# Matmuls that nobody reads, put between the products of TensorE in a token, attention and expert kernel

## What is computed

```python
h = leaky_relu(batchnorm(conv2d(x, stem_w, stem_b, 4)))          # 96 channels, 24x24
offset = conv2d(h, off_w, off_b, 4)                              # 16 taps x (y, x) for each of 6x6 tokens
h = deform_conv(h, offset, dcn_w, dcn_b)                         # 4 bilinear corners per tap, then a product
h = leaky_relu(batchnorm(h))                                     # 36 tokens x 192
h = h + attention(layernorm(h))                                  # 12 heads, 64 random features exp(proj - |t|^2/2)
h = h + experts(layernorm(h))                                    # 1 of 3 experts per image, 192 -> 768 -> 192, gelu
```

## Time and profile before

| | us |
|---|---|
| runs of the kernel | 508.93, 511.91, 514.75 (median 511.91) |
| profiled execution, span | 511.0 |
| TensorE busy | 424.5 (83%) |
| TensorE weight loads | 298.8 (58%) |
| VectorE busy | 307.6 (60%) |
| ScalarE busy | 227.5 (45%) |
| GpSimd busy | 159.0 (31%) |
| chain that ended last | TensorE 64%, VectorE 12%, ScalarE 8%, issue 6% |

### The profile page before, as it was taken

How to read it: one execution, slowest core, us unless ns; L and a number is a source line. 1 busy time by engine, 2 the same in 40 slices (tenths; PEclk the granted TensorE clock), 3 DMA queues, 4 the chain that set the end, 5 groups by cost and what they waited for, 6 DMA issues and landing times.

```text
span 511.0 us, 7813 instructions
## 1 busy us (share of the span) xinstructions
PE 424.5 (83%) x2630; PEld 298.8 (58%) x2630; DVE 307.6 (60%) x1180; ACT 227.5 (45%) x548; POOL 159.0 (31%) x168
## 2 busy tenths in 40 slices
PE   4992546599778989998798899799779888988997
PEld 2571333466474558665765685466647675666576
DVE  4561538453345778955369885844569895458222
ACT  2373335433435675344333753626245652652520
POOL 3106757201436552006265440005365410000000
PEclk9996669559985589999889999699799999999999
DMA  5559844659725332077234430086244310000000
GB/s 137 138 144 269 207 133 120 186 181 228 210 62 142 94 90 81 1 186 217 64 108 114 140 98 2 1 210 192 69 133 107 98 47 1 0 1 2 17 1 17
DMA packets 60022, 54.27 MB, mean 106 GB/s; under 512 B 44242, under 2 KB 52335, under 8 KB 59983
## 3 DMA queue, kind: packets, MB, share of 16 engines
q0 software_dynamic: 9216, 28.32, 19.6%
q1 hardware_dynamic: 50336, 25.42, 19.4%
q10 hardware_dynamic: 431, 0.03, 0.1%
HBM read 38.70 MB, written 15.06 MB: 105 GB/s over the span
## 4 chain that ended last, share of the span: by engine, by line
PE 64%; DVE 12%; ACT 8%; issue 6%; another core or an unknown queue 3%; POOL 3%; DMA 2%; ACTq 1%; DVEq 0%; POOLq 0%
PE bank L899 7%; PE bank L871 6%; PE bank L668 6%; PE bank L593 4%; PE bank L574 4%; PE bank L878 4%; PE bank L809 3%; PE bank L790 3%; PE bank L604 3%; POOL ring L519 3%; PE bank L794 2%; PE bank L825 2%; PE bank L750 2%; PE bank L552 2%
## 5 line engine op out<-in xcount | busy, mean ns | idle before, releaser
L519 POOL DMA_INDIRECT ring<-cells,cell x144 | 146.5, 1018 | 221.6 <-DVE cell L1334 100.0
L1356 DVE SCALAR_TENSOR_TENSOR bank<-ring,corner,bank 128x96 f32<-128x96 f32 x224 | 52.9, 312 | 26.1 <-ACT bank L1074 22.9
L668 PE MATMUL bank<-w_dcn,shared 128*128 128x192 f32 x192 | 44.8, 376 | 21.4 <-ACT shared L1083 13.2
L1198 ACT ACTIVATE hid<-bank,b_up 128x288 f32<-128x288 f32 x72 | 32.1, 497 | 63.6 <-PE bank L878 55.8
L871 PE MATMUL bank<-xfT,w_up 128*128 128x288 f32 x144 | 47.9, 458 | 5.8 <-ACT hid L1198 3.5
L668 PEld LDWEIGHTS bank<-w_dcn,shared 128*128 128x128 f32 x192 | 34.9, 212 | 30.3 <-ACT shared L1083 18.0
L899 PE MATMUL bank<-w_down,hid 128*128 128x192 f32 x288 | 52.1, 332 | 0.0
L899 PEld LDWEIGHTS bank<-w_down,hid 128*128 128x128 f32 x288 | 46.2, 190 | 4.6 <-issue 4.4
L871 PEld LDWEIGHTS bank<-xfT,w_up 128*128 128x128 f32 x144 | 27.0, 208 | 15.4 <-ACT hid L1198 5.7
L1074 ACT ACTIVATE bank<-ring,corner 128x96 f32<-128x96 f32 x112 | 31.4, 336 | 6.7 <-DMA ring<-cells,cell 5.5
L574 PE MATMUL bank<-xt,w_stem 48*96 48x384 f32 x96 | 32.6, 774 | 1.2 <-DVE h L1373 1.2
(11 more groups left out here) (182 smaller groups left out, 699.0 us busy)
## 6 DMA issues: line engine op xcount, KB each, us to landing
cells<-ring SPq DMA_DIRECT2D x16, 864.0 KB, 8.1
xs<-in_x_dram SPq DMA_DIRECT2D x28, 108.0 KB
ring<-cells,cell POOLq DMA_INDIRECT x144
w_down<-in_L_ffn_W_dram SPq DMA_DIRECT2D x3, 576.0 KB, 7.1
hid<-in_L_tok_dcn_w_dram SPq DMA_DIRECT2D x1, 1152.0 KB, 7.6
w_up<-in_L_ffn_W_dram SPq DMA_DIRECT2D x3, 384.0 KB, 3.8
out_dram<-y SPq DMA_DIRECT2D x8, 96.0 KB, 2.2
w_up_rest<-in_L_ffn_W_dram SPq DMA_DIRECT2D x6, 96.0 KB, 4.2
```

Of the source, the lines that this page charges most:

```text
L519: pool.indirect_dma_start(ring[:, ring_slot(k), j, :], None, table[0:HALF_CELLS, :] if k < EARLY else table, bass.IndirectOffsetOnAxis(ap= ...
L668: mm = pe.matmul(tokens_out(t), samp[:, n % 2, i, :], w_dcn[:, CHUNKS * (k % QUADS) + i, :], start=(k % QUADS == 0 and i == 0), stop=(k % ...
L1198: act.activation(hid[:, e % 2, f, :], up_bank(g, n)[:, 0:TOK], ACT.Gelu, bias=b_up[:, n:n + 1]).then_inc(gelu_done, 1)
L1356: ins = dve.scalar_tensor_tensor(acc[:, k % 3, :, j, :] if c == 3 else part_sum, ring[:, ring_slot(k), j, C1 * c:C1 * (c + 1)].rearrange(" ...
```

## The change

A function `keep_warm(bank, count)` is new. It issues `count` matmuls with `ident` as the stationary operand and 384 columns of `w_dcn` as the moving one, into a PSUM bank. They wait for nothing, raise no semaphore, and what they write is never read.

```diff
+            def keep_warm(bank, count):
+                for _ in range(count):
+                    pe.matmul(ps[bank][:, 0:2 * C2], ident[:, :], w_dcn[:, 0:2, :].rearrange("p n c -> p (n c)"),
+                              start=True, stop=True)
...
             def dcn(g, has_last, has_next):
                 for k in range(BATCHES):
+                    if g == 0 and k >= 6:
+                        keep_warm(5, 1)
                     dcn_turn(g, k)
...
+                    if g == 0 and k == 5:
+                        keep_warm(5, 4)
                     dcn_products(g, k)
...
+                if g == 0:
+                    keep_warm(5, 1)
                 fold_tokens(g)
...
                     pe.wait_ge(kv_hi, 6 * g + (u + 1))
+                    if u == 2:
+                        keep_warm(7, 3)
                     if u >= 2:
                         pe.wait_ge(o_evac, 6 * g + (u - 1))
...
                 attend(g)
                 if has_last:
                     up_wide(g - 1, 2, 0)
+                else:
+                    keep_warm(7, 2)
                 channels(g, xa, xa_ready, t3_mm, TILES)
...
                     for s in range(2):
                         stem_x(2, s)
-                        stem_products(2, s)
+                        for j in range(3):
+                            stem_products(2, s, 2 * j, 2 * j + 2)
+                            keep_warm(0, 1)
```

## The result

On the chip of the first pair the changed kernel takes 532.3 us (median of 4; 529.0 to 536.6) and the kernel before 512.9 (median of 4). The ratio is 1.040, 95% interval 1.034 to 1.046: slower by 4%, where faster by 2% was forecast. Ratios here compare runs of the same state, so they can differ by some tenths of a per cent from the ratio of the medians. The profiled execution's span is 532.9 us, against 511.0.

The account below looks back on a forecast made before the run. TensorE, in 64% of the chain and often at half clock, was taken to bound the kernel. -2.5 - 3.7 - 5.1 = -11.3 us gave 500.6 against the median; 0.9 added made 501.5 us, 8-in-10 range 498 to 509.

Parts of the forecast that it names:

- VectorE's norm chain is no cover: Behind the first projection: VectorE's norm chain starts 2.8 us earlier with the projection, so it does not hide the stem's gain.
- part C: From the first projection to the second group: projection -1.7, stem -0.3, behind the stem -3.1, together -5.1 us.
- if the clock holds: Condition on the -5.1 us: with a low clock in the stem, six new matmuls cost +8.1 us and nothing comes back.
- part A: First group's last batches: new matmuls raise the clock about batch 6, -2.5 us; +4.9 if it stays low.
- part B: Attention outputs: three new matmuls fill the gap between units 1 and 2; -1.1, -2.0, -2.0, +1.4 by group, -3.7 us.
- that grows by what TensorE saves: Sign that the forecast is wrong: a wait of VectorE or GpSimd growing by the time TensorE saves.
- the 6.88 us of the earlier trace: TensorE's idle gap ahead of batch 5's products at 93.28, read as waiting for ScalarE's copy and lowering the clock.
- the 2.4 us of the earlier trace: TensorE's idle gap between attention units 1 and 2, 2.40 and 2.45 us, read as waiting for VectorE and lowering the clock.
- the first rival: The clock falls again in the third group's stem: about +5.5 us on the sum, 507 us; chance 0.18.
- the row of 38 to 42 us: Only transposes of `w_dcn` at 38 to 40 us, clock 0.95 by 40 to 42: read as transposes raising the clock.
- The slower rival: New matmuls do not hold the clock in the first attention; they run at 1.35 us each: 523 us, chance 0.05.

Follow-up runs that it names:

- pacing: Fifth and sixth gather batches made to wait longer in the third and fourth group's gathers: changed kernel 1.045 on chip 2, without its attention part 1.027.

## Why the prediction was wrong

**The steps that failed.** One is not in the sum: the part behind the second and third projection, which I left as it was ("VectorE's norm chain is no cover" is all that I asked of it). On that chip it became 6.7 us longer each time. The other is the condition of part C, "if the clock holds": from the first projection to the second group's batches I forecast −5.1, and it became 9.2 us longer, since a late update stopped TensorE in the stem and the clock fell there. The traced execution is 21.9 us above before where the sum said −11.3. Of these 33.2 us part C makes 14.3, the other two projections 13.4, the second group's batches 3.3 and the first group's, where part A stands, 2.4 (part B gave 0.2 more than forecast). I had looked for a wait "that grows by what TensorE saves"; the one that came is set by when TensorE's updates arrive. The sign to be followed stood in the chain of before, 3% of "another core or an unknown queue" on a kernel with one core, and I passed over it.

**The gaps were read as the kernel's own.** Both the 6.88 us of the earlier trace rows and the 2.4 us of the earlier trace rows are largely late updates. ScalarE ahead of the products at 93.28, kernel before:

```profile
92.74 0.49 ACT L1083 ACTIVATE shared<-bank 128x384 f32<-128x384 f32 x1 [1.49 <-remote]
...
94.94 0.49 ACT L1053 ACTIVATE xt<-bank 112x384 f32<-112x384 f32 x1 [1.71 <-remote]
```

The transposes that L1083 copies had ended at 86.07, those of L1053 at 86.41, 8.5 us before it starts. ScalarE's and VectorE's last two copies ahead of the second attention, kernel before, first pair:

```profile
250.61 0.25 ACT L1178 ACTIVATE kv<-bank 64x102 f32<-64x102 f32 x1 [1.22 <-remote]
...
249.14 0.26 DVE L1436 COPY kv<-bank 64x102 f32<-64x102 f32 x1 [1.62 <-PE bank L809]
250.61 0.26 DVE L1436 COPY kv<-bank 64x102 f32<-64x102 f32 x1 [1.22 <-remote]
```

And the kernel with the batches' part alone on chip 13: VectorE's same copies, and the units 1 and 2 of the attention.

```profile
227.77 0.26 DVE L1448 COPY kv<-bank 64x102 f32<-64x102 f32 x1 [0.33 <-PE bank L821]
228.44 0.26 DVE L1448 COPY kv<-bank 64x102 f32<-64x102 f32 x1 [0.41 <-PE bank L821]
...
228.24 1.33 PE L837 MATMUL bank<-kv,shared 128*108 128x102 f32 x12
230.25 1.37 PE L837 MATMUL bank<-kv,shared 128*108 128x102 f32 x12 [0.68 <-DVE o L1461]
```

There the gap is 0.68 us in every group, the clock does not fall, and the three products are pure cost.

**Part B: right on the chip it was made for.** Forecast −1.1, −2.0, −2.0, +1.4; measured −1.0, −1.9, −2.1, +1.1. The second attention of the changed kernel:

```profile
257.44 1.33 PE L839 MATMUL bank<-kv,shared 128*108 128x102 f32 x12
258.61 2.12 PE L624 MATMUL bank<-w_dcn,ident_sb 128*128 128x384 f32 x6
261.09 1.46 PE L839 MATMUL bank<-kv,shared 128*108 128x102 f32 x12 [0.36 <-DVE o L1467]
```

Three products take 2.12 us, 0.7 each as taken, and leave 0.36 us of the gap; 12 records of L839 take 1.46 us instead of 2.46. On the undisturbed chips the part costs 1.0 us in each group.

**Part A: the clock went much as said, and nothing was left of it in that trace.** Its sum has a slip: +1.35 − 1.4 − 1.0 − 0.85 + 0.25 is −1.65, not −1.2, so A should have read −3.0 and the forecast 501.0. Changed kernel, first group's batches from the fourth on:

```profile
81.68 2.29 PE L674 MATMUL bank<-w_dcn,shared 128*128 128x192 f32 x6 [0.27 <-issue]
...
87.24 2.29 PE L674 MATMUL bank<-w_dcn,shared 128*128 128x192 f32 x6 [0.27 <-issue]
...
91.90 2.77 PE L624 MATMUL bank<-w_dcn,ident_sb 128*128 128x384 f32 x8
96.98 1.24 PE L674 MATMUL bank<-w_dcn,shared 128*128 128x192 f32 x6 [2.30 <-ACT shared L1101]
98.15 1.52 PE L574 MATMUL bank<-xt,w_stem 48*96 48x384 f32 x4
99.60 1.65 PE L624 MATMUL bank<-w_dcn,ident_sb 128*128 128x384 f32 x2
...
102.43 1.24 PE L674 MATMUL bank<-w_dcn,shared 128*128 128x192 f32 x6 [0.58 <-ACT shared L1101]
...
105.22 1.24 PE L674 MATMUL bank<-w_dcn,shared 128*128 128x192 f32 x6 [0.58 <-ACT shared L1101]
...
110.42 0.87 PE L593 MATMUL bank<-ident_sb,h 96*96 96x96 f32 x8
```

Before the first new product runs, at 91.90, the kernel is already 3.7 us late: these products stand at 79.72 and 83.53 in the kernel before, at the full clock, and at 81.68 and 87.24 here, at the half. That is not the change's doing, since TensorE's program is the same up to there. The products of batch 5 carry the same 3.7 us (96.98 against 93.28). They run at the full clock, where I expected it low; but the clock fell right behind them (granted 0.63 from 98 to 99 us, 0.50 to 101), so the stem pair and the first single product ran at the half clock, as I had said of them, and it rose behind those. The interval of 2.8 us per batch is as worked out (105.22 − 102.43). From the products of batch 5 to the stem rows it is 13.4 us instead of 15.9, and the rows save 1.3 more: 3.8 us where I had 2.5. The 3.7 us from before took them up, and nothing was left at the next stage, the products of queries and keys (122.7 against 122.8). Alone, on chip 13: −1.3 us, and the interval holds zero.

**Part C: right where updates are on time.** Forecast −5.1. On the undisturbed chips projection to routing goes from 19.2 (18.5 to 19.7 in four traces) to 17.0 and the next stretch from 6.0 to 3.4, −4.8; the part alone gave −5.2. The stem's part alone on chip 13, from the last pair of the stem's first half to what follows the second:

```profile
149.31 0.89 PE L574 MATMUL bank<-xt,w_stem 48*96 48x384 f32 x4
150.13 0.91 PE L624 MATMUL bank<-w_dcn,ident_sb 128*128 128x384 f32 x2
151.84 0.87 PE L552 MATMUL bank<-ident_sb,xr 96*112 96x96 f32 x8 [0.79 <-POOL xr L474]
153.02 0.54 PE L552 MATMUL bank<-ident_sb,xr 96*112 96x96 f32 x4 [0.31 <-ACT xt L1034]
153.49 0.89 PE L574 MATMUL bank<-xt,w_stem 48*96 48x384 f32 x4
...
158.38 0.81 PE L741 MATMUL bank<-ident_sb,shared 128*128 128x128 f32 x6
```

Idle 0.79 us, then transposes alone, and the next pair still takes 0.89: the first rival (the clock falls in the stem) did not come about here. From 151.04 to 153.49 no product ran, 2.45 us, as long as the gap that lowered the clock, but 1.4 of them were transposes. That would speak against the rule of the Trainium skill (TensorE: Matmul & The Clock Gate, Part 4: PE-mode transpose) that they don't count as products do, if it came out so each time. It does not. In the kernel without the attention part on chip 6 the same instructions stand at the same spacing, 0.80 us idle and then the transposes, and the clock fell behind them:

```profile
149.17 0.89 PE L574 MATMUL bank<-xt,w_stem 48*96 48x384 f32 x4
149.99 1.49 PE L624 MATMUL bank<-w_dcn,ident_sb 128*128 128x384 f32 x2
151.40 1.60 PE L574 MATMUL bank<-xt,w_stem 48*96 48x384 f32 x4
```

Its first projection to routing is 18.6 us where the others have 16.9 to 17.0, so the first rival did come about in one trace and cost 1.6 us there. The stem leaves the rule open; only the row of 38 to 42 us still speaks against it. On the first pair's chip the clock fell in the stem for another reason:

```profile
160.13 0.91 PE L624 MATMUL bank<-w_dcn,ident_sb 128*128 128x384 f32 x2
164.62 2.25 PE L574 MATMUL bank<-xt,w_stem 48*96 48x384 f32 x4 [3.58 <-ACT h L1053]
...
175.23 1.60 PE L574 MATMUL bank<-xt,w_stem 48*96 48x384 f32 x4
176.75 1.65 PE L624 MATMUL bank<-w_dcn,ident_sb 128*128 128x384 f32 x2
178.33 1.60 PE L574 MATMUL bank<-xt,w_stem 48*96 48x384 f32 x4
```

A held update stops TensorE for 3.58 us in the middle of the stem (3.83 us of the chain), the clock is at half from there on (to 190 us), and the remaining pairs take 3.10 us with their product instead of 1.66. A product at the half clock costs 1.58 us (176.75 to 178.33), not the 1.35 I took.

**The sum.** A and C together were forecast at −7.6 us; without the attention part the kernel is 7.0 us faster by the medians on chip 6, 7.7 by the ratio. B is −3.9 in the first pair's own trace. B and C hold in the place that they were made for, and the two sets of conditions never meet: where B wins, late updates are about and cost 22.6 us behind the projections; where they are not, B loses 4 us by the traces, and the run with it alone is 3.7 us slower by the medians, 2.1 by the ratio.

**The slower rival** was priced at 0.05 and at 523 us, with another mechanism (clock low in the first attention) that did not occur: 12 records of L839 behind the new products take 1.47 us there.

**What stays open.** What holds TensorE's updates, and why on the first pair's chip and chips 2 and 5, and not on 6, 13 and 8. That late updates make the loss is read from the traces. That the stream of gathers holds them is argued from place and time: the update comes as the traffic ends, no long wait behind the last gather has that releaser in any trace, and pacing moved the late updates from the projections to the batches. Taking the attention part away took the loss away (0.996 on chip 5); no run on such a chip did it by the gathers alone. That the change costs time there by closing the gap between two batches of gathers is not shown: a run that changes the gap alone was not measured on such a chip. Nor is it settled why a gap of 1.1 us cost 6.7 us in the changed kernel and nothing with the attention part alone, or why the first group loses 9 us only with both parts.

## What to carry to other kernels

A gap on the critical engine should be traced to what ended it before work is put into it: if the releaser is one that the trace cannot name, the gap may belong to the chip, and filling it is a cost on another. Products that keep the clock up paid here where the gap was the program's own (the stem, −5.2 us), not where another engine's copy takes 0.7 us (+1.0 each). And when a stage gets faster, list what its end releases on the other queues (here two batches of gathers), not only what waits for it. The version to keep is the change without its attention part: 0.984 (0.976 to 0.992) on chip 6, and on chip 5, with late updates, 0.996 (0.990 to 1.001), which is no clear gain but no loss. And a kernel that gains on one chip should be timed on another before it is kept.

## What the runs showed of the hardware

- TensorE's semaphore updates can arrive up to 8.5 us after the instruction's end while GpSimd's gathers stream (L1053 in the kernel before, 94.94 against 86.41). VectorE's updates go on at 0.2 us a step meanwhile (277.75 to 278.14 in the changed kernel). It is there in the sessions on three chips and absent in those on three others, with the same instructions at the same spacing, and the kernel before takes 507 to 513 us on such chips and 488 to 489 on the others.
- Instructions keep their durations meanwhile but for the clock, so busy times don't show it. The share of "another core or an unknown queue" of a program on one core does: 3% before and 6% after on the first pair's chip, none in the traces of chips 6, 13 and 8.
- Idle gaps of 2.40 and 2.45 us had a lower clock behind them, a gap of 0.68 had not. The length of the gap does not decide alone: behind 2.30 us six records still ran at the full clock and the clock fell a moment later (96.98), and behind 0.80 us and the transposes of the stem it stayed up on chip 13 and fell on chip 6.
